# A chunk order of its own for each head group of a causal attention kernel, with a rising walk in the first group

## What is computed

```
xn = _layernorm(x, axis=-1)                      # x: (2, 2048, 256)
Q, K = _rope(Q), _rope(K)                        # (2, 16, 2048, 16)
scores = jnp.einsum('bhnd,bhmd->bhnm', Q, K) * scale
scores = jnp.where(causal, scores, -jnp.inf)
out = jnp.einsum('bhnm,bhmd->bhnd', jax.nn.softmax(scores, axis=-1), V)
x = x + (out @ Wout + bout) + moe(xn)
```

## Time and profile before

| | |
|---|---|
| median of 3 runs | 1004.11 us (998.84 to 1004.76) |
| span of the profiled execution | 1022.0 us |
| busy: PE, DVE, ACT, POOL | 89%, 83%, 71%, 45% of the span |
| `project`, until the first item | 0 to 136.4 us |
| front | 136.4 to 177.7 us |
| groups 0 and 1 | 177.7 to 268.0, to 361.3 us |
| groups 2 to 5 | to 470.1, 578.7, 687.0, 794.6 us |
| groups 6 and 7 | to 887.4, to 978.1 us |
| `output` | to 1022.0 us |

### The profile page before, as it was taken

How to read it: one execution, slowest core, us unless ns; L and a number is a source line. 1 busy time by engine, 2 the same in 40 slices (tenths; PEclk the granted TensorE clock), 3 DMA queues, 4 the chain that set the end, 5 groups by cost and what they waited for, 6 DMA issues and landing times. The chain is left out here.

```text
span 1022.0 us, 22104 instructions
## 1 busy us (share of the span) xinstructions
PE 907.5 (89%) x7874; PEld 392.7 (38%) x7874; DVE 847.0 (83%) x1096; ACT 728.5 (71%) x1542; POOL 462.9 (45%) x588
## 2 busy tenths in 40 slices
PE   2888446999999999999999899999999999999888
PEld 1554311332432334344434444344434333322257
DVE  6999789899899878886889688877888799894846
ACT  3556200788788878787888788778878788789822
POOL 4677568565201253344833474354132245355610
PEclk8999755999999999999999999999999999999979
DMA  9766810301200324244413542255334321112113
GB/s 324 267 248 248 276 46 11 105 3 38 68 2 2 115 78 121 76 133 147 125 53 98 151 143 74 72 162 132 77 85 125 90 62 49 32 58 64 37 52 124
DMA packets 82084, 106.65 MB, mean 104 GB/s; under 512 B 10000, under 2 KB 59064, under 8 KB 80952
## 3 DMA queue, kind: packets, MB, share of 16 engines
q1 hardware_dynamic: 74488, 85.83, 26.1%
q0 software_dynamic: 6528, 17.83, 6.8%
q10 hardware_dynamic: 960, 1.57, 0.5%
HBM read 67.37 MB, written 37.50 MB: 103 GB/s over the span
## 5 line engine op out<-in xcount | busy, mean ns | idle before, releaser
L1275 DVE TENSOR_REDUCE blk<-psP 128x2 f32<-128x1024 f32 (+2 forms) x576 | 641.4, 1162 | 103.5 <-PE psP L1421 53.7
L1221 ACT ACTIVATE probs<-psS 128x512 f32<-128x512 f32 (+3 forms) x1280 | 589.2, 541 | 162.2 <-PE psS L1458 153.1
L1458 PE MATMUL psS<-Qs,Ks 50*128 50x512 f16 (+3 forms) x1280 | 332.0, 353 | 24.5 <-ACT probs L1221 15.4
L1418 PE MATMUL psP<-Ks,Qs 48*128 48x512 f16 (+3 forms) x1280 | 299.6, 363 | 31.7 <-DVE blk L1275 20.5
L1514 PE MATMUL psO<-probs,Vs 128*32 128x512 f32 (+3 forms) x2560 | 300.3, 547 | 6.0 <-POOL probs L1124 4.9
L1124 POOL TENSOR_SCALAR_AFFINE_SELECT probs<-probs 128x512 f32<-128x512 f32 x128 | 88.1, 689 | 356.3 <-ACT probs L1221 317.4
L1458 PEld LDWEIGHTS psS<-Qs,Ks 50*128 50x128 f16 x1280 | 96.4, 93 | 256.6 <-ACT probs L1221 149.2
L1418 PEld LDWEIGHTS psP<-Ks,Qs 48*128 48x128 f16 x1280 | 80.4, 94 | 132.9 <-DVE blk L1275 94.8
L1421 PE MATMUL psP<-later,eye 64*128 64x128 bf16 x1024 | 103.6, 223 | 0.0
L1514 PEld LDWEIGHTS psO<-probs,Vs 128*32 128x32 f32 x2560 | 52.9, 108 | 86.4 <-issue 65.2
L1421 PEld LDWEIGHTS psP<-later,eye 64*128 64x128 bf16 x1024 | 78.1, 98 | 19.6 <-issue 1.7
(11 more groups left out here) (170 smaller groups left out, 729.3 us busy)
## 6 DMA issues: line engine op xcount, KB each, us to landing
xn<-we_scratch SPq DMA_DIRECT2D x72, 256.0 KB
expert_scratch<-xn SPq DMA_DIRECT2D x36, 256.0 KB
v_scratch<-vst SPq DMA_DIRECT2D x8, 1024.0 KB, 4.0
qk_scratch<-part SPq DMA_DIRECT2D x32, 256.0 KB, 4.0
Vs<-v_scratch SPq DMA_DIRECT2D x16, 512.0 KB, 3.9
Qs<-qk_scratch SPq DMA_DIRECT2D x168, 32.0 KB
Ks<-qk_scratch SPq DMA_DIRECT2D x168, 32.0 KB
acc<-x SPq DMA_DIRECT2D x8, 512.0 KB, 9.2
```

The costliest lines, as they stand in the source:

```text
L1221: nc.scalar.activation(probs[u % NPR][:, h, q0:CH], psS[:, k % SB, q0:CH], ACT.Exp, scale=exp_scale).then_inc(s_read[k % SB], 1)
L1275: nc.vector.tensor_reduce(out, src, AX.X, ALU.max).then_inc(item_ok[slot], 1)
L1418: ins = pe.matmul(psP[:, slot, at:at + w], Qs[r][rows, qt // CT, p, t * P:(t + 1) * P], Ks[r][rows, kc, p, 0:w], start=True, stop=True)
L1458: pe.matmul(psS[:, k % SB, q0:CH], Ks[r][rows, kt // CT, p, kt % CT * P:(kt % CT + 1) * P], Qs[r][rows, c, p, q0:CH], start=True, stop=Tru ...
```

## The change

Each kind of group gets a walk of its own (`WALKS`), and a list of the chunks whose maxima it computes (`QUEUE`). In fact all keep (3, 2, 0, 1) but the first, which walks 0, 1, 2, 3. `FIRST = (0,)`: only chunk 0's 6 items stand in front; group 0 computes the maxima of its chunks 1, 2, 3 between its own units, and then those of chunks 3 and 0 of group 1, 102 items in all. Group 1 keeps its chunks and items but has an order string of its own. The strings of `experts`, `behind` and `last` are untouched.

```diff
-        WALK = (3, 2, 0, 1)
-        FREED = {2: 1, 1: 0}
+        KINDS = ("start", "route", "experts", "behind", "last")
+        WALKS = {'start': (0, 1, 2, 3), 'route': (3, 2, 0, 1), 'experts': (3, 2, 0, 1), 'behind': (3, 2, 0, 1), 'last': (3, 2, 0, 1)}
...
+                self.freed = {self.ends[max(at(2), at(3))]: [1]}
+                self.freed.setdefault(NU - 1, []).append(0)
...
-        first_items = with_m([(1, 3), (1, 0)], None)
+        FIRST = (0,)
+        QUEUE = {'start': [(0, 1), (0, 2), (0, 3), (1, 3), (1, 0)], 'route': [(0, 2), (0, 1), (1, 3), (1, 0)], 'experts': [(0, 2), (0, 1), (1, 3), (1, 0)], 'behind': [(0, 2), (0, 1), (1, 3), (1, 0)], 'last': [(0, 2), (0, 1)]}
+        first_items = with_m([(0, c) for c in FIRST], None) + [("m", 0, FIRST[-1])]
...
         PE_ORDER = {
-            "plain": (
-                    "ss10s01sspms10ss1s0s10s1ss01s0sp10sss01p01ssp01sss10ps10ssp01sss10pss0s10s1sp0ss1ps0s110sspss100"
...
+            "start": (
+                    "1010010101s101sss01s0100s1ps0101s011001ss01psm10s0s110sss1s0p0ss1p10ss0ss1s0s101ssss01s0s1p10ss0"
...
+        TABLES = 8
...
+        FETCH = 33
...
-            for n in range(TILES):
+            made = TABLES
+            for n in range(TABLES):
                 tables(n)
...
-                        if g == 1 and u == ends[1]:
+                        if (g, u) == (1, FETCH):
```

More of the change, by code:

```diff
@@ L869, in attend @@
         added = sem("added")
-        WALK = (3, 2, 0, 1)
-        FREED = {2: 1, 1: 0}
+        KINDS = ("start", "route", "experts", "behind", "last")
+        KIND = ["start", "route"] + ["experts"] * 4 + ["behind", "last"]
+        WALKS = {'start': (0, 1, 2, 3), 'route': (3, 2, 0, 1), 'experts': (3, 2, 0, 1), 'behind': (3, 2, 0, 1), 'last': (3, 2, 0, 1)}
         def tiles(c):
@@ L944, in attend @@
         }
-        cuts = [n for n, x in enumerate(PE_ORDER["plain"]) if x == "m"]
-        PE_ORDER["route"] = PE_ORDER["plain"][:cuts[0]] + "r" + PE_ORDER["plain"][cuts[0]:cuts[1]] + "r" \
-            + PE_ORDER["plain"][cuts[1]:]
         def order_of(kind):
             more = kind != "last"
-            queue = with_m([(0, 2), (0, 1)] + ([(1, 3), (1, 0)] if more else []), (0, 0))
+            before = KIND.index(kind) - 1
+            queue = with_m(QUEUE[kind], (0, QUEUE[KIND[before]][-1][1]) if before >= 0 else None)
             if not more:
-                queue.append(("m", 0, 1))
-            order, ns, nv, half, pairs = [], SB, 0, None, dict(x=0, y=0, r=0)
-            outs = [("o", 0, c) for c in WALK]
+                queue.append(("m",) + QUEUE[kind][-1])
+            order, ns, nv, half, pairs = [], SB if before >= 0 else 0, 0, None, dict(x=0, y=0, r=0)
+            outs = [("o", 0, c) for c in WALKS[kind]]
             for x in PE_ORDER[kind]:
@@ L1078, in _ @@
             load_v(0, 0, 1)
-            n = first_items.index(("m", 1, 3))
-            store_m(n % 2, n // 2, 0, 0, 3)
+            for n, x in enumerate(first_items):
+                if x[0] == "m":
+                    store_m(n % 2, n // 2, turn_of(0, x), 0, x[2])
             load(1, 1, 1)
@@ L1099, in _ @@
                             load_e(buf, EG * (g - 2) + x[1] + 2)
-                    elif x[0] == "pv" and x[1] in ends and units[x[1]][0] in FREED and g < GROUPS - 2:
+                    elif x[0] == "pv" and (x[1] in walk[g].freed and g < GROUPS - 2 or (g, x[1]) == (1, FETCH)):
                         u = x[1]
@@ L1104, in _ @@
                         sp.sem_inc(carrier, 1)
-                        load(g + 2, r, FREED[units[u][0]])
-                        if g == 1 and u == ends[1]:
+                        for half in walk[g].freed.get(u, []):
+                            load(g + 2, r, half)
+                        if (g, u) == (1, FETCH):
                             sp.wait_ge(ids_ok, ONE + 1)
@@ L1169, in _ @@
                     split(0)
-                for x in [("s", 0, i) for i in range(SB)] + orders[KIND[g]]:
+                for x in ([("s", 0, i) for i in range(SB)] if g else []) + orders[KIND[g]]:
                     if x[0] == "s" and x[2] == HG - 1 and x[1] < NU:
                         u = x[1]
-                        if diag[u] is not None:
+                        if walk[g].diag[u] is not None:
                             mask(g, u)
-                        if g == 0 and u in SPOTS[:TILES]:
+                        if (g, u) in TABLES_AT:
                             passed(g, u)
-                            tables(TILES + SPOTS.index(u))
-                        if g in (3, 4) and u in SPOTS[:TT]:
-                            t = (g - 3) * TT + SPOTS.index(u)
+                            for n in range(made, made + TABLES_AT[g, u]):
+                                tables(n)
+                            made += TABLES_AT[g, u]
+                        if g in (3, 4) and u in walk[g].spots[:TT]:
+                            t = (g - 3) * TT + walk[g].spots.index(u)
                             nc.gpsimd.tensor_tensor(acc[:, t, :], acc[:, t, :], bo[:, :], ALU.add).then_inc(bout_ok, 1)
-                        if g == 1 and u == ends[1]:
+                        if (g, u) == (1, FETCH):
                             pool.wait_ge(ids_ok, ONE + 1)
@@ L1207, in body @@
             def body(g):
-                    order = orders[KIND[g]]
+                    order, ends, q0s = orders[KIND[g]], walk[g].ends, walk[g].q0s
                     def copy_out(n):
@@ L1226, in probabilities @@
                             copy_out(CHUNKS - 1)
-                    for i in range(SB):
+                    for i in range(SB if g else 0):
                         probabilities(0, i)
@@ L1461, in _ @@
             pe.wait_ge(one_rows, ONE + 16 * 2 * SIDES)
-            for i in range(SB):
-                scores(0, 0, 0, 0, i)
             def turn_x(g, x):
@@ L1499, in body @@
                     j, r = divmod(g, 2)
-                    order = orders[KIND[g]]
+                    order, diag, at_walk = orders[KIND[g]], walk[g].diag, walk[g].chunks.index
                     def pv(u):
-                        c, kt = units[u]
-                        q0, end = q0s[u], u in ends
+                        c, kt = walk[g].units[u]
+                        q0, end = walk[g].q0s[u], u in walk[g].ends
                         if diag[u] is None:
```

102 lines of the change are left out of this document (52 added, 50 removed).

## The result

The changed kernel takes **1026.07 us** (median of 4 runs, 1024.45 to 1026.65) against 1004.2 us for the kernel before (998.84 to 1004.76). The ratio is 1.0217 with a 95% interval of 1.019 to 1.0245: slower by some 22 us. The prediction of 1002 us and its range of 991 to 1011 were wrong.

What follows compares the result with a forecast made beforehand. DVE's full queue was taken to bound the front and group 0, leaving only its idle time to win. Terms -3.0 + 1.0 + 0.7 - 1.0 = -2.3 us took 1004.1 to 1002 us, range 991 to 1011.

Steps and rivals of the forecast that it cites:

- Rival 2: Front and group 0: the front was idle time after all, so units start earlier; -27 us, 977 us, chance 0.02.
- the closer packing: Group 0: its 57 full reductions packed as tightly as the front's would give 1.8 us back; taken as 0.
- the first rival: Front, groups 0 and 1: the mix removes DVE's idle time; -11.6 us, 992.7 us, chance 0.11.
- The step on group 1's own order: Group 1 and its end: a new order of the same items and units gives -1.0 us, bounds -5 and +3.0.
- Scores and exponentials from about 148 us: Front and group 0: units starting earlier than 177.7 us cut DVE's idle time; -3.0 us, bounds 0 and -6.8.
- The term for moving 30 items: Front into group 0: the move itself costs nothing, covered by DVE's own full queue; taken as 0.
- this sign of being wrong: Front and group 0: the forecast is wrong if the order leaves `psP` empty on full items; no size given.
- the step on TensorE's clock: Front and group 0: the clock rises near 155 us instead of 183, worth 0 since DVE is slower at either level.
- The first turn: Chunk 0's copy to `nmT` in the front: nothing queued hides the transposition; +1.0 us, bounds 0.3 and 1.2.
- The second store: Chunk 1's start in group 0: its store waits behind 50 loads on SP; +0.7 us, bounds 0 and 3.
- Taking "what comes after" as unchanged: After 361.3 us, from group 2 on: same orders as before, so its 660.7 us stay unchanged.
- Rival 3: Chunk 1's start and group 1's end: units wait at both joints, with a slower turn; +7.2 us, 1011 us, chance 0.13.

## Why the prediction was wrong

**The reading of what bounds the front held.** DVE does the same work from 136.4 us to the end of group 0, 123.9 and 123.5 us, and the closely packed front was no idle time. Rival 2 was rightly set aside. One reading in it was wrong without consequence: two of the 29 reductions in the earlier trace rows are the shorter `128x768` ones. The front's 28 full ones were busy 31.9 us, 1.139 each, so the closer packing, priced at 1.8 us in the first rival, is worth 0.9 at most. That rival's 992.7 us, too, is 992.5 when added up as the forecast is (1004.1 - 11.6).

**The step on group 1's own order failed, and with it the forecast.** I put -1.0 us with bounds of -5 to +3. It cost 13.2 us in group 2, less 0.7 gained in group 1. Of the 13.2 us SP's order makes 7.8, the turn's place on PE and DVE 2.3, and the bare items 3.1. After the change, the copy for the next group's first chunk stands behind the last value products. I had read what this means for PE, DVE and ACT (the five bare items, +3.0, which the runs put at +3.1), but not for SP. SP walks the same string, stops at unit 39 and issues 25 loads before it comes to the store. The prediction did that very sum for SP at the start and for the end of group 0, but not for the one place where the store after the loads is the next thing that anyone waits for. By its own rows it was there to be had: 12 loads in 4.18 us make 25 loads some 8.7 us, where SP's order alone gave 7.8 back. The moved turn, SP's order alone, and the new order on the old start all put the cause there.

**The step "Scores and exponentials from about 148 us" failed: -3.0 us was +8.** The exponentials began at 150.37 us, nearly when expected. The share that I wanted back from the heads partly came (1.7 us of waiting in front of their `128x768` reductions against 2.9). But the full items waited 8.8 us for PE, and DVE was busy 89% of the stretch, where I had written above 94%. The term for moving 30 items, "nothing, the cover being DVE's own full queue", falls with it: beside units, at the low clock, the queue was not full. The prediction had named this sign of being wrong itself (`psP` empty on full items). No run moves the items without the units, so the 8 us can't be split between the two terms.

**Behind it stands the step on TensorE's clock, "this is worth 0 here".** I expected 1.0 from about 155 us; the changed kernel's row over 148 to 177.2 has 0.56 and the next 0.79. I had written that a clock that stayed low with units beside the items would make PE's work the bound, and gave it neither a price nor a chance. The runs show the mechanism in both orders: in the old one, less work for PE, clock 0.50 from 195 to 220 us, 3.9 us lost in group 0; in the new one, 1.27 and 1.13 us of waiting for PE where the clock dips and none where it does not.

The Trainium skill (page "TensorE: Matmul & The Clock Gate", Part 1) says that the clock depends on how busy the engine has been of late. The trace agrees on the fall: with the value products cut, the clock left 1.00 in a stretch in which PE was busy 3.67 us of 5 (190 to 195 us). It doesn't agree in any simple way on the return: the clock then stayed at 0.50 for 25 us in which PE was busy 24.77. The prediction left the rule out, though the change spreads PE's work more thinly: over 177.2 to 207 us PE is busy 85% of the time, where the kernel before has 95% from 195 to 220.

What stays open: no run held the clock at 1.00 from 150 us on, so how much of the 8 us the clock accounts for is not measured, and why it doesn't rise for good before 183 us isn't either.

**The smaller terms.** DVE of the changed kernel in order of time, 136 to 180 us (as the earlier trace rows):

```profile
144.97 0.21 DVE L1293 COPY nmT<-psP 32x128 f16<-32x128 f16 x1 [0.40 <-PE psP L1439]
145.91 0.69 DVE L1290 TENSOR_REDUCE blk<-psP 128x4 f32<-128x512 f32 x1 [0.73 <-PE psP L1431]
...
166.92 0.21 DVE L1293 COPY nmT<-psP 32x128 f16<-32x128 f16 x1 [0.76 <-PE psP L1439]
```

and SP's rows in the same stretch (as the earlier trace rows):

```profile
164.16 0.58 SPq L1094 DMA_DIRECT2D wo<-wout  x1
167.16 1.28 SPq L1066 DMA_DIRECT2D Qs<-nmT  x2
```

*The first turn*: DVE waited 0.40 us before the copy, against +1.0; the 0.73 after it is a head's wait, which another term had already counted. *The second store*: SP was free at 164.7 us and the copy came at 166.92, so the backlog cost 0 and not 0.7; SP was 0.9 us earlier than estimated (165.6), and the copy later than I had it. The 2.0 us that the prediction cites for such a store are given in the Trainium skill (page "DMA: Bandwidth & Descriptors", section on the anatomy of one DMA) for DMAs that GpSimd issues, and SP issues this one; no term hangs on them. Nor are the 3.2 us from copy to score a bound elsewhere: at group 2's start it was 3.8 us from the store's issue to the first score. *Tables*: no wait shows in the changed kernel; two to a unit cost some 6 us. *The fetch at unit 33*: 0 in the new order; group 1 lost 3.4 us in the old, with the tables in it. *Group 2's 50 loads*: 0.

**Taking "what comes after" as unchanged failed twice.** Group 2's string is untouched, but its first store is written in group 1's. And the 660.7 us were read from an execution 18 us above the timed runs; I noted the ratio of 0.9825 and did not ask where the 18 us lay. Against the second profile 15.2 us stand in groups 2 to 5 (433.3 us against 418.1). This didn't make the miss, but it let the span of 1024.6 look like no change.

**Rival 3** had the side on which the result fell. Its +3.0 us for the bare items came true, and with them its condition: group 1 took 90.9 us against 91.6, so its units about kept their pace. The rest did not: SP's backlog at chunk 1's start cost nothing, and the turn 0.4 us and not 1.2. That its side came true is in good part luck, since it had neither SP's queue at the end of group 1 nor the clock in group 0, which make most of the loss.

## What to carry to other kernels

- Where several engines walk one order, read each move on every one of them, and on a DMA-issuing engine above all: list what it issues and waits for between the producer and the urgent transfer, at each joint of the program. Here 25 loads ahead of one store cost more than all that the change was about.
- Before taking load off TensorE, look at the clock rows. A stretch that another engine bounds while PE is 95% busy at full clock may become PE's when PE is given less to do.
- Compare the profiled span, and the repeating stages in it, with the timed runs before taking a profile as the yardstick; profile the kernel before a second time.

## What the hardware showed that I had not expected

- **Less work made the stretch longer.** With value products cut, the granted clock was 0.50 in place of 1.00 at 195 to 220 us, PE went from 9.48 to 10.00 us busy of 10 at 210 to 220, and group 0 took 3.9 us longer, counted from the first reduction.
- **A full PE did not bring the clock back at once.** In that run the clock stayed at 0.50 over those 25 us with PE busy 24.77.
- **A dip of the clock moves between executions of the same orders.** 0.75 at 215 to 220 us and 1.00 at 240 to 245 in one, 1.00 and 0.76 in the other; DVE waited 1.27 us at the one dip and 1.13 at the other.
- **A high clock does not carry over.** After 0.96 over 127 to 136.4 us, brought about by products of no use, it was 0.59 in the next 8.6 us and 0.50 from 145 on, with PE busy 6.47 us of 8.6 and then 14.86 of 20.
- **Issuing costs SP some 0.34 us for each DMA** (12 in 4.08 us), so that 25 loads held a store for 8.7 us, though the DMA engines were busy only 49% of the time meanwhile.
- **The same orders took different times.** Group 7 took 84.8 or 89.8 us in executions of the same orders. Groups 2 and 3 took 108.8 and 108.6 us in one profile and 103.4 and 104.8 in the next.
